# Key block 0 loaded by halves of its rows on two queues, and five idle products instead of six, in a graph attention kernel

## The reference, cut to what matters

```python
h = jnp.maximum(_layernorm(x, axis=-1), 0.0)
output = einsum('bni,io->bno', h, weight)
q = einsum('bni,io->bno', h, wq)
k = einsum('bni,io->bno', h, wk)
alpha = einsum('bno,bmo->bnm', q, k)
alpha = maximum(alpha, 0.0) * (adj != 0)
alpha = softmax(alpha, axis=1)
return x + einsum('bnm,bmo->bno', alpha, output)
```

## Time and profile before

| what | us |
|---|---|
| median of three runs | 412.74 |
| the profiled execution, its own time | 412.91 |
| its span, from the first to the last instruction | 411.1 |
| TensorE busy (share of the span) | 405.3 (99%) |
| VectorE busy | 298.1 (73%) |
| ScalarE busy | 277.7 (68%) |
| GpSimd busy | 264.7 (64%) |

### The profile page before, as it was taken

One profiled execution on the slowest core, in us unless ns is written; L12 is line 12 of the kernel. 1 busy time (PEld: TensorE's weight loads), 2 busy tenths in 40 slices (PEclk: granted clock), 3 DMA queues, 4 the chain that ended last, 5 costly groups with the idle time before them and its releaser, 6 DMA issues.

```text
span 411.1 us, 9529 instructions
## 1 busy us (share of the span) xinstructions
PE 405.3 (99%) x3580; PEld 321.7 (78%) x3580; DVE 298.1 (73%) x571; ACT 277.7 (68%) x592; POOL 264.7 (64%) x286
## 2 busy tenths in 40 slices
PE   8999999999999999999999999999999999999995
PEld 5444545979797997979798897979889797979884
DVE  5797789896867676776767777676777667656565
ACT  4749887765867677766777776776867777644534
POOL 0767896979495866759395775939577584910004
PEclk9999999999999999999999999999999999999999
DMA  8973858989889897997969498985978599493022
GB/s 284 373 110 67 217 103 217 232 205 217 181 208 191 245 155 212 189 204 188 192 212 196 156 214 199 197 218 173 198 241 158 156 220 181 75 197 112 2 104 102
DMA packets 161641, 75.03 MB, mean 183 GB/s; under 512 B 135360, under 2 KB 143808, under 8 KB 161600
## 3 DMA queue, kind: packets, MB, share of 16 engines
q1 hardware_dynamic: 161168, 73.81, 77.6%
q10 hardware_dynamic: 432, 0.66, 0.4%
HBM read 24.12 MB, written 16.78 MB: 99 GB/s over the span
## 4 chain that ended last, share of the span: by engine, by line
PE 90%; DVE 4%; DMA 2%; ACT 1%; SPq 1%; issue 1%; POOL 0%; DVEq 0%; POOLq 0%
PE bank L1166 10%; PE bank L1165 10%; PE bank L1163 10%; PE bank L1181 10%; PE bank L1180 10%; PE bank L1178 10%; PE s_bank L1192 3%; PE s_bank L1193 3%; PE s_bank L1194 3%; PE bank L1199 2%; PE bank L1200 2%; PE bank L1201 2%; PE bank L1320 2%; PE bank L1322 2%; PE bank L1321 2%; DMA x_sb<-in_x 2%
## 5 line engine op out<-in xcount | busy, mean ns | idle before, releaser
L423 POOL TENSOR_TENSOR hn_lo<-h,hn_hi 128x512 f16<-128x512 f32 x64 | 74.0, 1166 | 53.1 <-ACT hn_hi L554 52.9
L544 ACT ACTIVATE h<-x_sb,shift,rstd 128x512 f32<-128x512 f32 x64 | 50.0, 804 | 24.0 <-POOL shift L418 23.6
L449 POOL TENSOR_TENSOR hn_lo<-s,hn_hi 128x512 f16<-128x512 f32 x56 | 63.3, 1163 | 0.3 <-ACT hn_hi L559 0.3
L1163 PE MATMUL bank<-hT_hi,mt_hi 128*128 128x256 f16 x224 | 61.1, 273 | 0.0
L1165 PE MATMUL bank<-hT_lo,mt_hi 128*128 128x256 f16 x224 | 61.1, 273 | 0.0
L1180 PE MATMUL bank<-wt_lo,hT_hi 128*128 128x256 f16 x224 | 61.1, 273 | 0.0
L1166 PE MATMUL bank<-hT_hi,mt_lo 128*128 128x256 f16 x224 | 61.1, 273 | 0.0
L1178 PE MATMUL bank<-wt_hi,hT_hi 128*128 128x256 f16 x224 | 61.1, 273 | 0.0
L1181 PE MATMUL bank<-wt_hi,hT_lo 128*128 128x256 f16 x224 | 61.1, 273 | 0.0
L559 ACT ACTIVATE hn_hi<-s 128x512 f16<-128x512 f32 x56 | 33.8, 625 | 25.6 <-POOL s L438 19.9
L1180 PE MATMUL bank<-w_lo,hT_hi 128*128 128x256 f16 x168 | 45.8, 273 | 0.0
(11 more groups left out here) (169 smaller groups left out, 1115.2 us busy)
## 6 DMA issues: line engine op xcount, KB each, us to landing
out_h<-x_sb SPq DMA_DIRECT2D x63, 256.0 KB, 2.1
x_sb<-in_x SPq DMA_DIRECT2D x15, 1024.0 KB, 5.5
adj_sb<-in_adj SPq DMA_DIRECT2D x16, 256.0 KB, 5.3
hn_hi<-in_L_gnn_wq SPq DMA_DIRECT2D x4, 256.0 KB, 5.6
x_sb<-in_x SPq DMA_DIRECT2D x2, 512.0 KB, 7.2
w_sb<-in_L_gnn_weight SPq DMA_DIRECT2D x2, 512.0 KB, 8.7
hn_lo<-in_L_gnn_wk ACTq DMA_DIRECT2D x2, 256.0 KB, 3.8
hn_lo<-in_L_gnn_wk SPq DMA_DIRECT2D x2, 256.0 KB, 3.7
```

The costliest lines, as they stand in the source:

```text
L423: nc.gpsimd.tensor_tensor(hn_lo[:, s, b], h[:, b], hn_hi[:, s, b], ALU.subtract).then_inc(h_split, 1)
L449: nc.gpsimd.tensor_tensor(low, s32[:, f], high, ALU.subtract).then_inc(s_split, 1)
L544: nc.scalar.activation(h[:, b], x_sb[:, s, b], ACT.Relu, bias=shift[:, b:b + 1], scale=rstd[:, b:b + 1]).then_inc(h_made, 1)
L1163: nc.tensor.matmul(o, bh[:, k, cols], ah[:, :, k], start=first and c == 0 and k == 0, stop=False, skip_group_check=True)
```

## The change

Block 0 of wk is loaded by two DMAs of 64 rows each: rows 0 to 63 from SyncE's queue and rows 64 to 127 from ScalarE's. Both count on the semaphore of block 0, so its waits (VectorE's and TensorE's) go up to 32. Behind its half SyncE issues blocks 1 and 3, and ScalarE block 2. TensorE runs five idle products instead of six.

```diff
-    WARM = 6
+    WARM = 5
...
-            for r in (0, 2):
+            sp.dma_start(wk_sb[:N // 2, 0], wk[:N // 2, :]).then_inc(wk_loaded[0], 16)
+            for r in (1, 3):
                 sp.dma_start(wk_sb[:, r], wk[r * N:(r + 1) * N, :]).then_inc(wk_loaded[r], 16)
...
-            for r in (1, 3):
-                act.dma_start(wk_sb[:, r], wk[r * N:(r + 1) * N, :]).then_inc(wk_loaded[r], 16)
+            act.dma_start(wk_sb[N // 2:, 0], wk[N // 2:N, :]).then_inc(wk_loaded[0], 16)
+            act.dma_start(wk_sb[:, 2], wk[2 * N:3 * N, :]).then_inc(wk_loaded[2], 16)
...
-                vec.wait_ge(wk_loaded[r], 16)
+                vec.wait_ge(wk_loaded[r], 32 if r == 0 else 16)
...
-                pe.wait_ge(wk_loaded[r], 16)
+                pe.wait_ge(wk_loaded[r], 32 if r == 0 else 16)
```

## The result

Median of the changed kernel 414.14 us (22 runs, 413.07 to 415.91), of the kernel before 412.74 (22 runs, 412.46 to 413.79): ratio 1.0034, 95% interval 1.0024 to 1.0044. The forecast of 412.8 in a range of 412.2 to 413.4 was wrong.

A forecast was written before the change was run, and what follows sets the result against it. Bound: the waits through x's landing, TensorE 0.30 us beside. TensorE's start -0.5 us and x's issue +0.45 us absorbed, x's landing +0.05: 412.91 to 412.96 us profiled, 412.8 on the median's scale; range 412.2 to 413.4.

The forecast's parts named there:

- What bounds the kernel: Start of the kernel: waits run from x's load through VectorE, GpSimd, ScalarE, VectorE to TensorE at 31.73; TensorE 0.30 us beside.
- x's landing: First half of the x load, landing at 10.29 us before: to come 0.05 us later (0.0 to 0.1).
- The 0.21 us of room at the w_top exchange: Weight-scale step: TensorE's w_top transpose at 16.08 us has 0.21 us of room before it becomes the late one.
- The landing of block 0: First key block of wk: lands at 3.45 us instead of 3.93, bounds 3.28 and 3.93; gain absorbed before 7.01.
- the rival of slow halves: Half-row loads of block 0 move at half rate, x lands up to 0.65 us later: 413.4 us; chance 9%.
- the dip goes: New load order avoids the 0.52 us dip in DMA flow (5.0 to 6.0 us), loads land earlier: 412.3 us; chance 8%.
- The later issue of x behind one more DMA: SyncE's queue: x issued at 4.0 us instead of 3.55, some 0.45 us later, hidden by a full DMA pipe.
- The clock: TensorE still at 1.2 GHz when M's products start at 8.23 us, costing 1.8 us, 1.6 arriving: 414.4 us; chance 6%.
- My "against" argument: Before TensorE's transposes: pause stays at 0.3 us and they start earlier, so no less work is done by 5.9 us.

The follow-up runs named there:

- e6: Changed kernel with block 0 cut by columns (128 rows x 256 columns on each queue) and six idle products: median 412.99 us.
- e5: Kernel before, six idle products, with whole blocks 0, 1, 3 on SyncE's queue and block 2 on ScalarE's: median 413.37 us.
- e14: Changed kernel again, unaltered, one single profiled execution: 415.24 us.
- e8: Changed kernel with three idle products instead of five: median 415.14 us, five of six runs above 414.5.
- e2: Changed kernel with six idle products instead of five: median 413.72 us, 2 of 11 runs above 414.5.
- e3: Changed kernel with seven idle products instead of five: median 413.56 us, 2 of 11 runs above 414.5.
- e13: Changed kernel with ten idle products instead of five: median 413.62 us, ratio 1.0023 to the kernel before, no run above 414.5.
- e1: Kernel before, its loads kept, with five idle products instead of six: median 413.56 us, ratio 1.0017.
- e11: Changed kernel with block 0 cut by columns and seven idle products: median 412.86 us, ratio 0.9999 to the kernel before.
- e10: Changed kernel with block 0 cut by columns instead of rows, five idle products kept: median 412.61 us, ratio 0.9997 to the kernel before.
- e9: Kernel before, six idle products and old order, with block 0 as two 64-row DMAs, both on SyncE's queue: median 415.47 us, ratio 1.0070.
- e16: Changed kernel again, unaltered, one single profiled execution: 416.91 us.

## Why the prediction was wrong, step by step

*What bounds the kernel* held in the main: the path through x's landing, and TensorE close beside it. In the lower group every row behind x moved with it. The 0.21 us of room at the w_top exchange did not hold as counted: in the kernel before, top_diag could start up to 0.45 us later and still end with the same hn_lo of GpSimd, and past that point it ends a whole hn_lo later.

*The landing of block 0* is the step that failed first, though this landing is not on the path by itself. I gave it bounds of 3.28 and 3.93 and took 3.45, from bytes and flow alone. Measured were 3.98 in the profile after (maxima at 4.00) and, by the start of VectorE's first maximum, 3.72 to 4.22 in the eight other profiles with its loads and any number of idle products. The unseen operation was the issue of a 64-row DMA, which I took to cost what a 128-row one costs or less. It takes 0.58 us against 0.40, ScalarE's issue of block 2 behind it 0.85, and block 2 lands at 6.6 instead of 5.3. e6 shows that with 128 rows the 3.5 us were right, with nothing moving before 2.0 us there either; how much of the 0.5 us is the issue and how much the lower flow was not separated.

*x's landing*, the only term of my sum that was not zero, I set at +0.0 to 0.1 us, and 0.65 only for a rival. Measured in the profile: +0.48. Over all profiles x's statistics start at 9.81 to 10.31 in the eight with 128-row loads alone and at 10.73 to 11.63 in the ten with 64-row loads. So the rival of slow halves had the size (413.4, lower group 413.07 to 413.64) with a reason that was only part right: the halves were slow to issue, and the loads behind them flowed more slowly too. The flow at the dip did rise, as the rival *the dip goes* had it, and was lost elsewhere. The rules of the Trainium skill weighed there, "SBUF — State Buffer", section "Door 1: The DMA port swizzle (why `[64,N]` ≈ `[32,N]`)", on the 64 partitions and "DMA: Bandwidth & Descriptors", section "Rules for kernel authors", against two disjoint halves, pointed the right way. Whether the ports are the cause no run shows; what was measured is the longer issue and the lower flow.

*The later issue of x behind one more DMA* was said to be hidden. e5 and e6 bear it out: issue at 4.01, statistics at 10.23 and 9.81.

*The clock* is the second step that failed: I put one idle product fewer at nothing and a late rise at 6% and 414.4. It came in half of the runs, at 415.1 in their middle. The way was as described, from the idle products through the transposes to w_top's as the late one; e14 shows it. The price was right by luck: I had half of M's products at half speed for 1.8 us, while in e14 the transposes are the slow ones (M starts 1.27 us later than in the profile after, and its first eight records lose only 0.24 us), and the exchange adds 0.81 us that I did not have. My "against" argument (TensorE has done no less by 5.9) did not hold: it had a pause ahead of block 0 of some 0.8 us instead of 0.27 in the profile after, and a second one before block 2 that I did not see. That fewer idle products bring the late rise more often is shown (e8, e2, e3, e13); which of the two pauses matters, and what decides it in one execution, stays open, since in e14 the first pause was only 0.5 us. And e1 shows that even with the old loads one idle product fewer costs 0.7 us in the median.

*The range* of 412.2 to 413.4 ended where one rival stood alone. The lower group sits just around that end (413.07 to 413.64), and the upper one is both rivals at once: 413.4 for the loads and 1.7 us more for the clock. I had given each a chance and their coming together none, though the late landing and the missing idle product both lengthen the same pause.

## What to carry to other kernels

The form of a transfer is an operation of its own: if the trace has no row of it, neither its issue nor what queues behind it can be taken from rows of another form. Cutting a load by columns kept all 128 partitions and landed the block 0.3 to 0.4 us earlier than the whole load (maxima from 3.52, 3.57 and 3.65 in e6, e11 and e10, from 3.96 before); cutting it by rows landed it on average no earlier (3.72 to 4.22) and delayed the loads behind it. It bought no time, though: e10 and e11 are within 0.1% of the kernel before. The number of idle products ahead of a start guards a path that may look free in one profile: the cost of one fewer appeared in the distribution of many runs, not in the single profile (e1's profile was 412.75, its median 413.56).

## What the runs showed of the hardware that was not expected

A 64-row DMA of 2 KB rows issued in 0.57 to 0.58 us on SyncE's and ScalarE's queues, in every profile that has it, against 0.40 to 0.41 for the first one of 128 rows; the 128-row DMA issued next took 0.56 to 0.58 on SyncE (after, e9) and 0.85 on ScalarE (after), against 0.41 to 0.45. With two 64-row DMAs in a row on one queue the block was complete 4.8 us after the first issue (e9), against 3.2 for a whole one.

The change from the lower to the upper clock, by the cadence of like instructions, came between about 3.9 us (e6) and 13.3 us (e16) in eighteen profiles of kernels that start alike, and at 5.6, 8.0, 8.9, 10.7 and 13.3 us in the five of one and the same kernel, the changed one. The printed granted clock was 1.00 on both sides of it (in e14 for 7 to 10 us as for 11 to 13): at the start the cadence of equal instructions tells the clock, not that column.

A VectorE instruction on 3 x 3 elements took between 0.22 and 1.18 us, by when it began: in each of the eighteen profiles it ended with the GpSimd instruction of 128 x 512 that was running beside it.
